# The low part of x for the split products: from VectorE to GpSimd, behind GpSimd's second sum for C

## What is computed

```python
u = (x @ in_proj_w.T).reshape(B, T, H, P)            # H = 8 heads, P = 64
sel = x @ sel_proj_w.T                               # B and C: 8 x 128 each, and dt, lam, theta
B_proj = apply_rope_cumangle(B_proj, cum_angle)
C_proj = apply_rope_cumangle(C_proj, cum_angle)
# for each t:
Bx_t = u_t[:, :, :, None] * Bp_t[:, :, None, :]
h = alpha * h + beta * Bx_prev + gamma * Bx_t
y_t = einsum('bhpn,bhn->bhp', h, Cp_t)
```

## Time and profile before

| | us |
|---|---|
| median of 3 runs | 595.39 |
| lowest, highest | 595.18, 598.25 |
| the profiled execution | 597.6 |
| its span, first to last instruction | 595.8 |

### The profile page before, as it was taken

The page is one execution under the profiler, slowest core; times in us unless marked ns, Lnnn a source line. Parts: engine busy times, 40 slices in busy tenths (PEclk is TensorE's granted clock), DMA queues, the critical chain, the costliest instruction groups (busy, mean ns, idle before and its releaser), DMA issues. The chain is left out here.

```text
span 595.8 us, 12817 instructions
## 1 busy us (share of the span) xinstructions
PE 521.4 (88%) x3932; PEld 435.3 (73%) x3932; DVE 470.9 (79%) x1093; ACT 479.9 (81%) x1477; POOL 433.6 (73%) x568
## 2 busy tenths in 40 slices
PE   4979999999999889899999898999999787879187
PEld 4867888888887777688887777788777665756085
DVE  5665577677767999997758999997559999954994
ACT  3799999999998987789998869699999889853101
POOL 7447777888778696977778786877768886954742
PEclk9989999999999999999999999999999999998669
DMA  8832122222111111133211121232211211000001
GB/s 191 234 101 64 59 77 98 60 81 89 49 59 61 60 50 35 61 95 96 60 38 59 61 61 54 66 96 95 72 50 39 69 62 65 21 19 2 0 1 36
DMA packets 52302, 39.35 MB, mean 66 GB/s; under 512 B 7302, under 2 KB 48011, under 8 KB 52235
## 3 DMA queue, kind: packets, MB, share of 16 engines
q1 hardware_dynamic: 45898, 35.39, 20.2%
q10 hardware_dynamic: 6336, 3.15, 1.8%
HBM read 33.44 MB, written 4.46 MB: 64 GB/s over the span
## 5 line engine op out<-in xcount | busy, mean ns | idle before, releaser
L937 ACT ACTIVATE turned<-ps,sct 128x128 f32<-128x128 f32 x376 | 110.2, 446 | 0.0
L922 ACT ACTIVATE turned<-ps,sct 128x128 f32<-128x128 f32 x368 | 102.9, 433 | 5.1 <-issue 4.3
L1282 DVE TENSOR_TENSOR_SCAN lmat<-arow,band 128x512 f32<-128x512 f32 x64 | 86.0, 1349 | 3.6 <-POOL band L651 3.6
L630 POOL TENSOR_TENSOR cn<-turned 128x256 f32<-128x256 f32 x64 | 54.9, 858 | 39.9 <-ACT turned L937 39.9
L1816 PE MATMUL ps<-cT,bT 128*128 128x128 f32 x512 | 71.4, 283 | 8.6 <-DVE state L1321 6.3
L1290 DVE TENSOR_TENSOR mmat<-ps,lmat 128x512 f32<-128x512 f32 x64 | 43.9, 686 | 44.0 <-PE ps L1816 43.8
L1816 PEld LDWEIGHTS ps<-cT,bT 128*128 128x128 f32 x512 | 64.1, 193 | 15.7 <-issue 14.5
L630 POOL TENSOR_TENSOR bn<-turned 128x256 f32<-128x256 f32 x64 | 51.9, 811 | 28.5 <-PE ps L1848 16.9
L828 ACT ACTIVATE area<-ps 128x256 f32<-128x256 f32 (+1 forms) x68 | 34.8, 568 | 39.9 <-PE ps L2049 14.3
L1721 PE MATMUL ps<-w_sel_hi,xt_hi 128*128 128x512 f32 x128 | 59.5, 465 | 1.6 <-ACT turned L937 1.6
L1848 PE MATMUL ps<-wu,bn 128*128 128x128 f32 x384 | 53.7, 283 | 3.5 <-DVE mmat L1290 3.4
(11 more groups left out here) (272 smaller groups left out, 1408.3 us busy)
## 6 DMA issues: line engine op xcount, KB each, us to landing
arow<-alpha_rows SPq DMA_DIRECT2D x32, 512.0 KB, 3.8
drow<-decay_rows SPq DMA_DIRECT2D x64, 128.0 KB, 3.0
area<-in_L_attn_a_x_dram SPq DMA_DIRECT2D x4, 512.0 KB, 6.6
xT_rows<-turned SPq DMA_DIRECT2D x4, 512.0 KB, 5.4
xt<-xT_rows SPq DMA_DIRECT2D x32, 64.0 KB, 2.5
area<-in_L_attn_a_x_dram ACTq DMA_DIRECT2D x6, 256.0 KB, 3.1
out_dram<-area ACTq DMA_DIRECT2D x6, 256.0 KB, 2.5
area<-L_attn_a_sel_proj_w_dram SPq DMA_DIRECT2D x2, 512.0 KB, 6.8
```

The costliest lines, as they stand in the source:

```text
L630: pool.tensor_tensor(out[:, 0], zc[:, 0], zs[:, 1], ALU.subtract)
L922: last = act.activation(dst[h][:, N * q:N * q + N], bank(BK_B)[:, N * q:N * q + N], ACT.Copy, scale=scalars(c, k)[:, at + HH * h + q:at + ...
L937: last = act.activation(dst[h][:, N * q:N * q + N], bank(BK_C)[:, N * q:N * q + N], ACT.Copy, scale=scalars(c, k)[:, at + HH * h + q:at + ...
L1282: dve.tensor_tensor_scan(lmat[h], arow[i2][:, HH * P * h:HH * P * (h + 1)], band[h], 0.0, ALU.mult, ALU.add).then_inc(l_dve, 1)
```

## The change

`x_low` moves from VectorE's even step to GpSimd's even step, directly behind `add_c`. The semaphore is renamed from `xl_dve` to `xl_pool`; those who wait for it (SyncE's load, the three projections) stay as they are. The subtraction waits for ScalarE's high part, now on GpSimd's queue. Tile 0's was on GpSimd already.

```diff
@@ GpSimd @@
+            def x_low(c, b):
+
+                pool.wait_ge(xh_act, NB * c + b + 1)
+                pool.tensor_tensor(xt_lo[b % 2], xt[b % 2], xt_hi[b % 2].bitcast(F32), ALU.subtract).then_inc(xl_pool, 1)
+
...
                     if ok(k, 1):
                         add_c(c, k)
+                    if ok(k + 2, 1):
+                        x_low(c, (k + 2) // 2)
                     at_span(pieces, c, k, 0.583, 0.833, first)
                     if ok(k) and has_state(c, k):
                         weigh_u(c, k)
@@ VectorE @@
-            def x_low(c, b):
-
-                dve.wait_ge(xh_act, NB * c + b + 1)
-                dve.tensor_tensor(xt_lo[b % 2], xt[b % 2], xt_hi[b % 2].bitcast(F32), ALU.subtract).then_inc(xl_dve, 1)
-
...
                     at_span(pieces, c, k, 0.31, 0.762, first)
-                    if ok(k + 2, 1):
-                        x_low(c, (k + 2) // 2)
                     at_span(pieces, c, k, 0.762, 0.857, first)
@@ TensorE and SyncE: the renamed semaphore, for example @@
-                pe.wait_ge(xl_dve, tile + 1)
+                pe.wait_ge(xl_pool, tile + 1)
```

More of the change, by code:

```diff
@@ L378, in hybrid_block @@
         rows_stored = sem("rows_stored")
-        xT_first, xT_stored, xh_act, xl_dve = sem("xT_first"), sem("xT_stored"), sem("xh_act"), sem("xl_dve")
+        xT_first, xT_stored, xh_act, xl_pool = sem("xT_first"), sem("xT_stored"), sem("xh_act"), sem("xl_pool")
         packed_done = sem("packed_done")
@@ L491, in tile_loads @@
                 if not (first_chunk(c) and b < 2):
-                    after(sp, xl_dve, tile - 1)
+                    after(sp, xl_pool, tile - 1)
                     sp.dma_start(xt[i2], xT_rows[tile]).then_inc(xt_in[i2], 16)
@@ L618, in _ @@
             pool.wait_ge(xh_act, 1)
-            pool.tensor_tensor(xt_lo[0], xt[0], xt_hi[0].bitcast(F32), ALU.subtract).then_inc(xl_dve, 1)
+            pool.tensor_tensor(xt_lo[0], xt[0], xt_hi[0].bitcast(F32), ALU.subtract).then_inc(xl_pool, 1)
             pool.wait_ge(pa, PA["mean"])
@@ L1735, in project_b @@
                 h, i2, n = k % 2, (k // 2) % 2, UNITS * c + k
-                pe.wait_ge(xl_dve, NB * c + k // 2 + 1)
+                pe.wait_ge(xl_pool, NB * c + k // 2 + 1)
                 after(pe, bs_act, n)
```

## The result

The changed kernel is slower. Its median is 600.20 us over 8 runs (598.59 to 602.09); the kernel before gave 596.65 us over 8 runs beside it. One of those 8 took 659.71 us and does not enter the ratio, which is 1.0049 with a 95% interval of 1.0026 to 1.0071. Measured once more with 12 runs it was 1.0041 (1.0017 to 1.0064). The forecast was a change of -0.2 us and a time of 595.2 us; the change came to +2 to +3 us.

The account below looks back on a forecast made before the run. VectorE was taken to bound the stretches where the move can pay, about 225 of 595.8 us. Middle terms +0.22 +0.41 -0.80 gave -0.17, rounded -0.2: 595.2 us against the median 595.39; range 592.5 to 598.9.

Parts of the forecast that it names:

- tiles 13 and 21: GpSimd's full queue delays its second attention product past 0.13 us of margin; VectorE goes on 0.13 to 0.33 us later.
- tile 10: Tiles 10 and 18: waiting for ScalarE's high part makes GpSimd's residual root 0.72 us late; costs 0.18 us each.
- Chunk 0: 68.5 to 128 us, recurrence only: GpSimd's 0.79 us wait for TensorE at 83.81 covers the added 0.46; counted 0.
- VectorE gets back 0.20: Tile 10: no subtraction at 158.89 between residual and statistics, so 0.52 of the root's 0.72 us delay is left.
- The port rival: A VectorE scan catches GpSimd's subtraction at five places, up to 0.98 us each: +4.7, 600.1 us; chance 0.12.
- -0.20: Second chunk, 195.10 us: VectorE's removed subtraction gains 0.20 us, before the wait for GpSimd's product.
- The -0.19 at tile 15: Second chunk, 243.21 us, after the product wait: VectorE's removed subtraction gains 0.19 us.
- -1.10 from 447 us on: Last full VectorE stretch: four gains, 0.31, 0.42, 0.18 and 0.19 us, if the product wait spares it; otherwise -0.5.
- TensorE's waits of 1.4 us: Two TensorE waits for VectorE's subtraction, in full stretches; counted nothing, 1.2 us for the low end.
- The signs named in advance: Subtraction near 0.46 us behind the second C sum; new 0.3 to 0.9 us VectorE wait at tiles 13, 21; limits that refute.

Follow-up runs that it names:

- the kernel with the work added: Kernel before plus one 128x128 subtraction of constants on GpSimd every even step from tile 1, VectorE keeping its own; ratio 1.0028, median 599.23 us.

## Why the prediction was wrong, point by point

The step that failed first is the one at tiles 13 and 21: the forecast ended with VectorE's wait for GpSimd's product (+0.13 to +0.33 us) and put the instructions behind it at nothing, where the runs show another 1.03 us two instructions later. The second is tile 10, where the path went to ScalarE's norm and its margin, and not to VectorE's own state update.

- **Chunk 0, counted 0.** It creeps by 0.26 us over the chunk, in front of the weighting of u; with the subtraction behind it the creep is gone. The idle time at 83.81 covered the sums for B, but not all that stood between.
- **Tile 10, counted +0.18, was +0.55.** The root's delay was right, 0.72 forecast and 0.74 measured. Two later steps failed. "VectorE gets back 0.20": it got 0.08, since the statistics read the residual, which ended at 158.97, 0.12 us before they began anyway; taking out an instruction gives nothing there if the next one waits for the one ahead. And I followed the delay to ScalarE's norm with its 0.34 us of margin, and not to VectorE's own next work, the state update at 161.06, behind which TensorE's scores began at 162.24 without idle time.
- **Tiles 13 and 21, counted +0.13 to +0.33 each, net of the gains.** As far as the wait, the step was right in kind and a little high: the wait was forecast at 0.3 to 0.9 us and is 0.47, and VectorE goes on 0.05 us later than ahead of tile 12, its two gains spent, because GpSimd's run was indeed released earlier (its second sum for C starts at 207.34, 0.04 later than before, while VectorE is 0.25 behind). The step that failed is that the forecast ended there. What is released at a new moment meets the other engine's work at a new distance, and two instructions later VectorE lost 0.8 us, then 0.23. It is the largest error: 1.0 us at tile 13, and as much at tile 21 in one profile of two.
- **The port rival.** The two engines holding each other up was named; its chance (0.12) was low and its argument wrong: I looked for GpSimd's subtraction being caught by a VectorE scan, at the place of the subtraction ("at tile 13 VectorE is at a reduction and at products with one input in PSUM"). What was caught is VectorE, by sums that were there before, 11 us later. Its time of 600.1 is near the result of 600.20 by luck: it had five places of 0.98 us, where two of about 1.03 count, and it stood on a base that was too low (the point on the range).
- **Tiles 12, 15, 23 and the last chunk.** -0.20 was -0.19. The -0.19 at tile 15 is hidden in the profile by the low clock; without it the variants show -0.68, and tile 23, counted nothing, gave -0.58: the `onorm` product went free there, a term that the sum lacked as well, with the other sign. -1.10 from 447 us on was -0.86 and -1.04, although VectorE waited 0.13 us for GpSimd's product at 477.90.
- **TensorE's waits of 1.4 us, counted nothing.** They are gone in the changed kernel, and no gain is seen for them: they lie in the full stretches, the long one at 472 us.
- **The range, 592.5 to 598.9,** was worked out about 595.39, a median of three; over 120 runs the kernel before has 597.86. Three runs of a kernel that scatters by 6 us with its clock were too few to hang 0.2 us on. This is half of the miss: on 597.86 the range would have reached 601.4 and held the result, but the change would still have been forecast at -0.2 us and measured at +2 to +3.
- **The signs named in advance.** The subtraction's median (455 ns), its place and the new wait came. The stretch from 143 to 184 us changed by 0.5 us, at the limit set, through tile 10; scans of over 1.5 us became fewer (14, not 18); GpSimd's waits for C shrank by 1.7 us. None of the signs looked past the wait at tile 13.

The Trainium skill (SBUF — State Buffer, section Who interferes with whom) has the first to issue hold the shared pair of ports as an exclusive lock, the other blocked until it is given back. The hold-up itself (0.95 us and more, against 0.42), the free row sums (1.21 us beside GpSimd's sums) and the caught copy (0.87 us) agree with that section. The 1.75 us do not follow from it: by the recorded starts VectorE was 0.05 us ahead of the first sum (0.06 by the rounded rows) and was passed by both.

## What to carry to other kernels

Work taken off a full engine was worth nothing here where that engine next waits for the other one, and the new wait fixes the distance at which the two meet afterwards; read on past the wait, to VectorE's next instruction with two SBUF inputs, before pricing it. In this kernel the moved instruction was best put behind every small thing that others wait for (the weighting and the root: 1.2 us), and left where it was in the few tiles where GpSimd's queue is full (2.5 us). Fit the times against the granted clock before comparing variants that differ by less than 1%.

## What the runs showed of the hardware

The length of VectorE's `onorm` product (128x256, two SBUF inputs) against the distance between its start and that of the first of GpSimd's two sums for B. The 17 profiles have 102 such products; the 59 in which the two starts lie this near:

| VectorE's start against the first sum | cases | its duration |
|---|---|---|
| 0.16 to 0.19 us ahead | 13 | 0.49 to 0.51 in all |
| 0.01 to 0.05 us ahead | 18 | 1.73 to 1.75 in 13, 1.05 in 3, 0.42 in 2 |
| 0.01 to 0.07 us behind | 20 | 0.94 to 0.99 in 18, 1.68 and 0.42 once each |
| 0.11 to 0.21 us behind | 8 | 0.83 to 0.89 in 4, 1.54 to 1.56 in 4 |

From the first line to the second, about 0.13 us of distance costs 1.2 us; 0.1 us more gives 0.8 back. The three lengths are its own 0.42 to 0.5, that plus one sum, that plus both. In the two cases of 0.42 us in the second line the sum was held up instead (0.97 and 0.99 us). In the kernels without added work on VectorE, a wait for GpSimd's attention product put VectorE 0.01 to 0.05 us ahead, in the worst line, in all 17 cases.

Two things in the same rows bear on it. In all 92 cases in which the product took more than its own 0.42 us it ends 0.28 to 0.30 us after the end of the GpSimd instruction that it waited for last; with its own 0.42 us it would have begun 0.14 us before that end. And ahead of the first sum GpSimd runs `band` (line 651, 1.04 us): in the first line `band` has 0.22 us left when VectorE's product starts, in 17 of the 18 cases of the second 0.08 to 0.09. It looks as if a start within the last 0.14 us of `band` comes too late to go between `band` and the sum; that is inferred, and one of the 17 (481.41 in the kernel with the work added, 0.42 us) does not follow it. The table is not the whole rule either: in the kernel with the subtraction made twice the product at 389.30 started 0.40 us ahead of the first sum, with 0.43 us of `band` left, and took 2.08 us, passed by both sums. That a blocked VectorE instruction can be passed by two of GpSimd's was new to me; in the last line of the table it happened in half of the cases at equal distances, and what decides there is not in these traces and stays open. So does why the changed kernel's tile 21 took 1.05 us in one profile and 1.74 in the other, both 0.04 us ahead.
